# Scale factors of the feed-forward weights made sixteen pairs earlier, and three small operations put in other places

## What is computed

```python
x = x + _layernorm(attn(_layernorm(x)))   # 32 heads of 128, RMS norm over all of q and of k, softmax, Wo
x = x + _layernorm(ffn(_layernorm(x)))
def ffn(x):                               # 8 experts of rank 16
    base = x @ W_base.T + b_base
    gate = softmax(x @ W_gate.T); thr = sigmoid(x @ W_thr.T + b_thr) / 8
    w = where(gate >= thr, gate - thr, 0); w = w / sum(w)
    h = einsum("nd,erd->ner", x, A)
    return base + 2 * einsum("ner,ne,eor->no", h, w, B)
```

## Time and profile before

| | |
|---|---|
| median of three executions | 1068.48 us (1067.88 to 1068.65) |
| the profiled execution | 1073.24 us, of it the profile's span 1071.4 us |
| TensorE busy | 1044.0 us, 97% of the span |
| VectorE, ScalarE, GpSimd busy | 821.3, 762.6, 761.5 us |
| mean granted TensorE clock | 0.993 of full speed |

### The profile page before, as it was taken

One profiled execution on the slowest core, in us unless ns is written; L12 is line 12 of the kernel. 1 busy time (PEld: TensorE's weight loads), 2 busy tenths in 40 slices (PEclk: granted clock), 3 DMA queues, 4 the chain that ended last, 5 costly groups with the idle time before them and its releaser, 6 DMA issues.

```text
span 1071.4 us, 19670 instructions
## 1 busy us (share of the span) xinstructions
PE 1044.0 (97%) x5649; PEld 551.4 (51%) x5649; DVE 821.3 (77%) x1824; ACT 762.6 (71%) x1582; POOL 761.5 (71%) x717
## 2 busy tenths in 40 slices
PE   8999999999999989999999999999999999999897
PEld 5444444444445645556555555555555555544454
DVE  7888766667746778766787887787887887888887
ACT  3676666666657776776787788687787788677756
POOL 2688978788868466775777877877778778645513
PEclk8999999999999999999999999999999999999999
DMA  6679765656664679866577887867878878776702
GB/s 239 172 238 273 258 221 197 230 206 228 205 137 139 199 177 241 236 157 177 138 163 206 183 163 199 165 177 187 194 167 186 197 185 173 210 164 148 186 22 80
DMA packets 312409, 198.86 MB, mean 186 GB/s; under 512 B 275456, under 2 KB 279424, under 8 KB 312320
## 3 DMA queue, kind: packets, MB, share of 16 engines
q1 hardware_dynamic: 304688, 194.24, 68.0%
q10 hardware_dynamic: 7632, 3.57, 1.3%
HBM read 94.98 MB, written 35.68 MB: 122 GB/s over the span
## 4 chain that ended last, share of the span: by engine, by line
PE 80%; DVE 8%; ACT 5%; issue 3%; DMA 2%; POOL 1%; SPq 0%; ACTq 0%; POOLq 0%; DVEq 0%
PE ps L1594 24%; PE ps L1595 23%; PE ps L1596 23%; PE ps L1786 3%; PE ps L1788 3%; PE ps L1787 3%; DVE pair_q L2515 3%; ACT ps L1288 2%; ACT pair_q L1297 1%; DMA pair_k<-pair_q 1%; DVE ps L2501 1%; ACT k_hi L1245 1%; DVE stats L2090 1%; DMA y<-x 0%; DVE ffn_top L2619 0%
## 5 line engine op out<-in xcount | busy, mean ns | idle before, releaser
L2515 DVE SCALAR_TENSOR_TENSOR pair_q<-ps,row_inv,pair_q 128x512 f16<-128x512 f32 x256 | 174.5, 745 | 68.6 <-ACT pair_q L1297 65.0
L1288 ACT ACTIVATE ps<-ps,neg_max 128x512 f32<-128x512 f32 x256 | 168.2, 657 | 76.1 <-DVE ps L2501 76.0
L1594 PE MATMUL ps<-xh,wa_hi 128*128 128x512 f16 x512 | 194.2, 379 | 0.0
L1596 PE MATMUL ps<-xh,wa_lo 128*128 128x512 f16 x512 | 194.2, 379 | 0.0
L1595 PE MATMUL ps<-xl,wa_hi 128*128 128x512 f16 x512 | 194.2, 379 | 0.0
L2501 DVE TENSOR_SCALAR_CACHE_REDUCE ps<-ps,score_down 128x512 f32<-128x512 f32 x256 | 177.0, 753 | 12.2 <-PE ps L1596 11.9
L1297 ACT ACTIVATE pair_q<-ps,row_inv 128x512 f16<-128x512 f32 x256 | 154.5, 688 | 7.8 <-DVE row_inv L2508 7.5
L742 POOL TENSOR_TENSOR acc<-acc,squares 128x512 f32<-128x512 f32 x120 | 151.5, 1284 | 1.6 <-ACT squares L1139 1.6
L1139 ACT ACTIVATE squares<-ps,q_k_bias,qk_down 128x512 f32<-128x512 f32 x128 | 99.3, 784 | 45.9 <-PE ps L1596 31.6
L733 POOL TENSOR_TENSOR qk_out<-q_s,qk_out 128x512 f16<-128x512 f32 x64 | 76.0, 1188 | 53.3 <-ACT qk_out L1148 53.3
L2300 DVE TENSOR_SCALAR qk_out<-ps,k_b,k_g 128x512 f32<-128x512 f32 x64 | 51.8, 809 | 77.1 <-ACT squares L1139 77.1
(11 more groups left out here) (310 smaller groups left out, 2578.3 us busy)
## 6 DMA issues: line engine op xcount, KB each, us to landing
q_k_scratch<-qk_out SPq DMA_DIRECT2D x64, 512.0 KB, 3.6
qk_in<-q_k_scratch SPq DMA_DIRECT2D x64, 512.0 KB, 3.7
wa_stage<-w_qk SPq DMA_DIRECT2D x32, 512.0 KB, 4.3
u_stage<-w_vo SPq DMA_DIRECT2D x32, 512.0 KB, 5.3
wo_stage<-w_vo SPq DMA_DIRECT2D x16, 512.0 KB, 5.2
x_first<-w_vo SPq DMA_DIRECT2D x12, 512.0 KB, 4.5
qk_tops<-qk_top_scratch ACTq DMA_DIRECT2D x27, 128.0 KB, 3.7
y<-x SPq DMA_DIRECT2D x8, 256.0 KB, 6.0
```

What stands on the lines that cost most here:

```text
L1288: act.activation(ps[:, SCORE + i, :], ps[:, SCORE + i, :], ACT.Exp, bias=neg_max[:, sl, i:i + 1], scale=-1.0, accum_out=row_sum[:, sl, i:i ...
L1594: pe.matmul(outp, lhs[0], rhs[0], start=first, stop=False)
L1596: return pe.matmul(outp, lhs[1], rhs[0], start=False, stop=last)
L2515: dve.scalar_tensor_tensor(out=pair_q[:, 1, i, :], in0=ps[:, SCORE + i, :], scalar=row_inv[:, sl, i:i + 1], in1=pair_q[:, 0, i, :], op0=AL ...
```

## The change

On VectorE, the four reductions are done after steps 11, 13, 14 and 15, on base weights that ScalarE loads for this alone into `wv_stage` (two transfers of 512 KB, issued by ScalarE in steps 12 and 14, `load_base`). The load into `wb_stage` in step 52 stays, so `W_base` is loaded twice. SP stores the results in step 49 and loads them in step 50. `last_factors` follows step 52 (`two_pairs` now calls it at `j == 4`). ScalarE's high parts of `W_base` move to the ends of steps 57 and 58, those of the other two to the end of step 60. GpSimd's six splits move into steps 57 to 62, one each. `scores_down` moves from behind the low halves to between `inverses` and the low halves, in every step. In step 2, `maxima` come before `low_wo(0)`, the low halves before `split_v`, and `low_wo(1)` after both.

```diff
@@ SP
+                if j == 1:
+                    sp.wait_ge(ffn_top_ready, 4)
+                    sp.dma_start(ffn_top_scratch[0], ffn_top[:, :]).then_inc(ffn_top_stored, 16)
+                if j == 2:
+                    sp.wait_ge(ffn_top_stored, 16)
+                    sp.dma_start(ffn_tops[:, :, :], ffn_top_scratch.broadcast_to([P, P, 4])).then_inc(ffn_tops_loaded, 16)
             for s in range(4):
                 step(PAIRS - 2, s)
-                if s == 1:
...
-                if s == 2:
...
@@ GpSimd
-            for s in range(4):
-                step(PAIRS - 2, s, 0, more=2)
-            step(PAIRS - 1, 0, 1, more=2)
-            step(PAIRS - 1, 1, 1, weights=False)
-            low_base(0)
-            low_base(1)
-            step(PAIRS - 1, 2, 1, prepare=False, weights=False)
-            low_base(2)
-            low_base(3)
-            step(PAIRS - 1, 3, 1, prepare=False, weights=False)
-            pool.wait_ge(inv_ready, 4 * PAIRS)
...
+            step(PAIRS - 2, 0, 0, more=2)
+            step(PAIRS - 2, 1, 0, late=low_base(0, 2 * PAIRS + 3))
+            step(PAIRS - 2, 2, 0, late=low_base(1, 2 * PAIRS + 4))
+            step(PAIRS - 2, 3, 0, more=4, late=low_base(2, 2 * PAIRS + 6))
+            step(PAIRS - 1, 0, 1, more=5, late=low_base(3, 2 * PAIRS + 8))
+            step(PAIRS - 1, 1, 1, weights=False, late=low_others(0, 2 * PAIRS + 9))
+            step(PAIRS - 1, 2, 1, prepare=False, weights=False, late=low_others(1, 2 * PAIRS + 10))
             step(PAIRS - 1, 3, 1, prepare=False, weights=False)
@@ ScalarE
+            def load_base(k):
+                act.wait_ge(wv_lo_ready, 8)
+                if k:
+                    act.wait_ge(ffn_top_ready, 2)
+                act.dma_start(wv_stage[:, :, :].rearrange("p c n -> p (c n)"),
+                              w_base[:, k:k + 2, :].rearrange("p c n -> p (c n)")).then_inc(wb_loaded, 16)
...
+            step(3, 0, 1, wo_parts(3, 1, 0), beside, part=formed(1, 1, 4))
+            load_base(0)
+            step(3, 1, 1, wo_parts(3, 1, 1), beside, part=formed(1, 1, 5))
+            step(3, 2, 1, wo_parts(3, 1, 2), beside, part=formed(1, 1, 6))
+            load_base(2)
+            step(3, 3, 1, wo_parts(3, 1, 3), part=formed(1, 1, 7))
...
+            after = (None, high_base(0, 1), high_base(2, 3), None)
             for s in range(4):
-                step(PAIRS - 2, s, 0, wo_parts(PAIRS - 2, 0, s), alone=s + 1)
+                step(PAIRS - 2, s, 0, wo_parts(PAIRS - 2, 0, s), alone=s + 1, build=after[s])
-            step(PAIRS - 1, 0, 1, high_base(0, 1), alone=5)
-            step(PAIRS - 1, 1, 1, high_base(2, 3), alone=6)
+            step(PAIRS - 1, 0, 1, nothing, alone=5, build=high_others)
+            step(PAIRS - 1, 1, 1, nothing, alone=6)
@@ VectorE, step
                 inverses(n, sl)
+                if down:
+                    scores_down(n + 1, 2 * p + (s + 1) % 2 + (2 if s == 3 else 0), 1 - sl, (s + 1) % 4 // 2)
                 for i in range(TB):
                     low_halves(n, sl, i)
...
-                if down:
-                    scores_down(n + 1, 2 * p + (s + 1) % 2 + (2 if s == 3 else 0), 1 - sl, (s + 1) % 4 // 2)
@@ VectorE, step 2
+            maxima(2, 0)
             low_wo(0)
-            maxima(2, 0)
-            low_wo(1)
             inverses(2, 0)
-            split_v(4, 6, YB)
             for i in range(TB):
                 low_halves(2, 0, i)
+            split_v(4, 6, YB)
+            low_wo(1)
             scores_down(3, 1, 1, 1)
@@ VectorE, later
             step(2, 3, 0, beside, part=formed(1, 1, 3))
             largest_of_last(2, in_loaded, 16, in_stage[:, :, :].rearrange("p c n -> p (c n)"))
+            step(3, 0, 1, beside, part=formed(1, 1, 4))
+            step(3, 1, 1, beside, part=formed(1, 1, 5))
+            largest_of_base(0)
+            step(3, 2, 1, beside, part=formed(1, 1, 6))
             largest_of_last(3, bt_loaded, 16, bt_stage[:, :])
+            step(3, 3, 1, part=formed(1, 1, 7))
+            largest_of_base(1)
...
-            two_pairs(FORMED, 0, largest_of_base)
+            two_pairs(FORMED, 0, last_factors)
```

More of the change, by code:

```diff
@@ L1058, in _, with low_base, low_others @@
             two_pairs(FORMED, 0, last=True)
[L1059 to L1079 removed]
+            def low_base(c, done):
+                return lambda: split_weights(ffn_hi_ready, ffn_lo_ready, c + 1, wb_lo[:, c, :], wb_stage[:, c, :],
+                                             wb_hi[:, c, :], wb_up[:, :], done)
+            def low_others(k, done):
+                lo, stage, hi, up = ((bt_lo[:, :], bt_stage[:, :], bt_hi[:, :], bt_up[:, :]),
+                                     (in_lo[:, :, 0:IN], in_stage[:, :, 0:IN], in_hi[:, :, 0:IN], ffn_by[:, 1:2]))[k]
+                return lambda: split_weights(ffn_hi_ready, ffn_lo_ready, C + 1 + k, lo, stage, hi, up, done)
+            step(PAIRS - 2, 0, 0, more=2)
[5 more added lines that the diff above has]
+            step(PAIRS - 1, 2, 1, prepare=False, weights=False, late=low_others(1, 2 * PAIRS + 10))
+            step(PAIRS - 1, 3, 1, prepare=False, weights=False)
             def add_ffn(t):
@@ L1465, in last_wv, with high_base, some, high_others @@
                 return some
+            def load_base(k):
[4 more added lines that the diff above has]
+                              w_base[:, k:k + 2, :].rearrange("p c n -> p (c n)")).then_inc(wb_loaded, 16)
+            def high_base(*chunks):
+                def some():
+                    act.wait_ge(ffn_by_ready, 1)
+                    act.wait_ge(wb_loaded, 64)
+                    for c in chunks:
+                        act.activation(wb_hi[:, c, :], wb_stage[:, c, :], ACT.Copy,
+                                       scale=wb_up[:, :]).then_inc(ffn_hi_ready, 1)
+                return some
+            def high_others():
+                act.activation(bt_hi[:, :], bt_stage[:, :], ACT.Copy, scale=bt_up[:, :]).then_inc(ffn_hi_ready, 1)
+                act.activation(in_hi[:, :, 0:IN], in_stage[:, :, 0:IN], ACT.Copy,
+                               scale=ffn_by[:, 1:2]).then_inc(ffn_hi_ready, 1)
             def two_pairs(c, odd, last=False):
@@ L1487, in _ @@
             step(2, 3, 0, wo_parts(2, 0, 3), beside, part=formed(1, 1, 3), build=building(1, 3))
-            for s in range(4):
-                step(3, s, 1, wo_parts(3, 1, s), beside if s < 3 else None, part=formed(1, 1, 4 + s))
+            step(3, 0, 1, wo_parts(3, 1, 0), beside, part=formed(1, 1, 4))
[4 more added lines that the diff above has]
+            step(3, 3, 1, wo_parts(3, 1, 3), part=formed(1, 1, 7))
             with act.Fori(1, FORMED // 2) as i:
@@ L1553, in norm_ffn @@
                                scale=rstd[:, 3, t:t + 1]).then_inc(ffn_normed, 1)
-            step(PAIRS - 1, 3, 1, nothing, prepare=False, between=high_others)
+            step(PAIRS - 1, 3, 1, nothing, prepare=False)
             for t in range(TB):
@@ L2622, in largest_of_base @@
             def largest_of_base(k):
[L2623 to L2642, removed]
-            two_pairs(FORMED, 0, largest_of_base)
+                largest_of_last(k, wb_loaded, 16 * k + 16, wv_stage[:, :, :].rearrange("p c n -> p (c n)"))
             def last_factors():
@@ L2660, in last_factors, with two_pairs @@
                                   ALU.mult, ALU.mult).then_inc(ffn_by_ready, 1)
-            step(PAIRS - 2, 0, 0, alone=1)
+            def two_pairs(c, odd, more=None):
+                for j in range(8):
+                    ends = more and j == 7
+                    step(2 * c + j // 4, j % 4, j // 4, part=None if ends else formed(c, odd, j), alone=0 if ends else None)
+                    if more and j == 4:
+                        more()
+            for s in range(4):
+                step(1, s, 1, plain, to=NT - 1 if s < 3 else None)
+            for s in range(3):
+                step(2, s, 0, plain)
+            step(2, 3, 0, beside, part=formed(1, 1, 3))
             largest_of_last(2, in_loaded, 16, in_stage[:, :, :].rearrange("p c n -> p (c n)"))
-            step(PAIRS - 2, 1, 0, alone=2)
+            step(3, 0, 1, beside, part=formed(1, 1, 4))
+            step(3, 1, 1, beside, part=formed(1, 1, 5))
+            largest_of_base(0)
+            step(3, 2, 1, beside, part=formed(1, 1, 6))
             largest_of_last(3, bt_loaded, 16, bt_stage[:, :])
-            step(PAIRS - 2, 2, 0, alone=3)
-            step(PAIRS - 2, 3, 0, alone=4)
-            last_factors()
+            step(3, 3, 1, part=formed(1, 1, 7))
+            largest_of_base(1)
+            with dve.Fori(1, FORMED // 2) as i:
+                two_pairs(2 * i, 0)
+                two_pairs(2 * i + 1, 1)
+            two_pairs(FORMED, 0, last_factors)
+            for s in range(4):
+                step(PAIRS - 2, s, 0, alone=s + 1)
             step(PAIRS - 1, 0, 1, alone=5)
```

15 lines of the change are left out of this document (removed).

## The result

| | kernel before | changed kernel |
|---|---|---|
| median | 1068.77 us (22 runs, 1067.15 to 1070.60) | 1070.27 us (22 runs, 1067.80 to 1073.22) |
| the profiled execution | 1073.24 us, span 1071.4 us | 1070.17 us, span 1068.4 us |

The ratio is 1.0014, with a 95% interval of 1.0008 to 1.0020: 1.5 us slower, where 1.8 us faster was forecast, and just above the range. Yet the two profiled executions differ by -3.0 us. Medians and profiles point in opposite directions, and that is the question of this study. The spread of the changed kernel is also wider (5.4 us against 3.5).

A forecast was written before the change was run, and what follows sets the result against it. TensorE was taken to bound the loop, VectorE's chain the end of attention. Part 1 at -4.0, part 2 at nothing and part 3 at +2.2 gave -1.8 us from 1068.48: 1066.7 us, range 1062.4 to 1069.8.

The forecast's parts named there:

- The bound and the tail: End of attention: VectorE's chain decides; without the added work, scores of step 56 to 62 take 54.5 us, not 60.3.
- the two port holds: Steps 59 and 60: GpSimd's splits hold up VectorE's `row_inv` at the shared port, 0.6 and 1.0 us, together +1.6.
- The last link, from step 62 to the end, stays as it is: After step 62: the stretch to the end of the kernel was forecast not to change.
- Step 53: the stop: Step 53: TensorE waits 2.2 us for a copy, because `last_factors` after step 52 makes VectorE's maxima 2.43 us later.
- a rival of its own with 0.16: Step 53: the clock falls behind the stop too, costing up to 1.5 us, total 1068.2; chance 0.16.
- Part 2: Every step: `scores_down` moves into a pause where VectorE waits for ScalarE; forecast to change nothing.
- part 1: End of attention: reductions moved to steps 12 to 16, `last_factors` after step 52, high parts and splits earlier; -4.0 us.
- Part 3: Step 2: VectorE's new order delays `low_wo(1)`, on which SP waits before issuing the transposes; +2.2 us, bounds +1.9 and +4.5.
- Landing then took 5.5 us and I keep that: Step 2: the low transposes were assumed to land 5.5 us after starting, as in the first profile.
- The wait of SP for `low_wo(1)`: Step 2: SP waits for `low_wo(1)` until 384.4, so the low transposes begin at 387.0, not 385.07, 1.9 us later.
- ScalarE's wait for the same load: Before step 3's exponentials: low halves of step 3 come at 393.5 to 394.5, ahead of what TensorE needs.
- The slower rival: Loop: `scores_down` held by GpSimd at most steps makes VectorE the bound, 44 steps cost 6.6 us, some 1071.3; chance 0.12.

The follow-up runs named there:

- a_step2_old: The changed kernel with step 2 in VectorE's old order; 1064.89 us, ratio 0.9961.
- a_sp_later: The changed kernel with `load_wo(0)` moved behind step 2 in SP's list; 1070.81 us, ratio 1.0021.
- the second profile of before: The kernel before, run again unchanged for another profile; 1068.97 us, ratio 0.9996, span 1068.3 us.
- b_down: The kernel before with only `scores_down` moved between `inverses` and the low halves in every step; 1067.38 us, ratio 0.9979.
- a_both_54: The changed kernel with `last_factors` after step 54 and, in step 2, `low_wo(0)` and `low_wo(1)` right behind `maxima`; 1063.52 us, ratio 0.9950.

## Why the prediction was wrong

**The bound and the tail: right.** VectorE's round against TensorE's 9.08 was read rightly. Six steps of 9.08 were forecast as 54.5 and are 54.48, in five kernels. Parts 1 and 2 together were forecast at -4.0 and measured -4.2 (-6.3 to -2.0). Counted from the scores of step 53, the forecast had the scores of step 62 at 85.9 us (989.6 - 903.73), and they came at 85.89 (990.98 - 905.09); the low halves of step 62 at best at 91.6 and with the two port holds at 93.2, and they came at 92.77. "The last link, from step 62 to the end, stays as it is" was right as well: from those low halves to the end of the span it is 1071.4 - 1000.87 = 70.53 us before and 1068.4 - 997.86 = 70.54 after.

The holds happened otherwise than forecast. Both fell in step 59, the second one on `scores_down`, each beside a subtraction on GpSimd:

```profile
968.71 1.16 POOL L837 TENSOR_TENSOR wo_lo<-wo_stage,wo_hi 128x512 f16<-128x512 f32 x1
968.89 1.00 DVE L2518 TENSOR_SCALAR row_inv<-row_rec 128x5 f32<-128x5 f32 x1
969.81 1.20 DVE L2411 TENSOR_SCALAR score_down<-rms,exp_scale 128x5 f32<-128x5 f32 x1
969.83 1.16 POOL L888 TENSOR_TENSOR k_lo<-qk_in,k_hi 128x512 f16<-128x512 f32 x1
```

TensorE did not stop for them: VectorE's low halves of step 58 had begun 2.9 us ahead of the scores that need them (960.83, 963.74), and those of step 59 still began 1.9 ahead (970.92, 972.82), where in the kernel before a lead of 0.9 was the one at which TensorE stood waiting (low halves of step 57 at 951.55):

```profile
952.44 0.38 PE L1594 MATMUL ps<-k_hi,qk_in 128*128 128x512 f16 x1 [0.63 <-DVE pair_q L2515]
```

But the lead did not come back. From there VectorE went round in 8.97 to 8.99 us up to step 62, on its own chain:

```profile
960.83 2.73 DVE L2525 SCALAR_TENSOR_TENSOR pair_q<-ps,row_inv,pair_q 128x512 f16<-128x512 f32 x4 [1.12 <-DMA pair_k<-pair_q]
970.92 2.71 DVE L2525 SCALAR_TENSOR_TENSOR pair_q<-ps,row_inv,pair_q 128x512 f16<-128x512 f32 x4
...
997.86 2.73 DVE L2525 SCALAR_TENSOR_TENSOR pair_q<-ps,row_inv,pair_q 128x512 f16<-128x512 f32 x4 [0.62 <-ACT pair_q L1293]
```

So the low halves of step 62 came 6.88 us after their scores and not 5.67: the term for the holds was 1.6, and 1.2 is what was lost (a wait of the low halves of step 58 for a transpose has a part in that, 0.5 us, which the forecast didn't have). Over all fourteen profiles the stretch from these low halves to the end is 70.1 to 70.7 us, while they came 6.9 to 8.1 us after their scores: the end goes with VectorE's chain, as the forecast assumed. No run takes the holds away, so their price at the end isn't shown by itself. The Trainium skill, SBUF — State Buffer, section SBUF: two separate sides, has VectorE and GpSimd lock one port pair for a whole instruction. The rows of step 59 agree with it.

**Step 53: the stop right, its price between two cases.** 2.2 was forecast, 2.01 to 2.23 measured in five profiles. In three the clock stayed up (12.57, 12.59, 12.80 us for the step), in two it fell and the step took 14.25 and 14.26. I had that as a rival of its own with 0.16; it is no either-or of kernels but of executions, 1.7 us in some of them: no profile of the changed kernel itself shows the fall, but `a_step2_old` and `a_sp_later`, which have the same step 53, do. That the changed kernel's times spread wider fits this; the timed runs have no trace, so it isn't shown for them. The Trainium skill, TensorE: Matmul & The Clock Gate, section Part 1: The HAM clock gate, says that the monitor runs free and doesn't start with the kernel. The five profiles are in keeping with that, though they don't prove it: stops of the same length, 2.01 and 2.02, came out both ways.

**Part 2: something alone, with part 1 not to be told.** I costed it at nothing and had its 0.14 us in part 1's round of 8.98. Alone it gives 2.2 us, all in the tail. Together with part 1 steps 56 to 62 went from 55.93 to 54.48, but the profile with both lost as much again to the clock in step 53 (14.25 against 12.80), and in the medians (ratios 0.9967 and 0.9961) no gain can be told.

**Part 3: the step that failed.** "Landing then took 5.5 us and I keep that", "The slow matmuls behind the stall stay", and, for the sum, "That execution lies 4.8 us above the median; the difference of two of them carries over". All three take the one profile of before for what the kernel usually does. It isn't: in it the low transposes of step 2 landed after 5.68 us; in four of the other five profiles with that order it was 4.07 to 4.14 us, TensorE stopped 0.78 to 0.86 us and the clock stayed up. So the usual kernel had neither the long stop nor the slow matmuls, and the change brings both. Against the second profile of before, 17.09 to 23.79 us:

```
stop before attend of step 2    4.85 - 0.86                                +4.0
12 matmuls of attend            (397.73 - 393.02) - (392.36 - 389.78)       +2.1
stop before rows (385.42)       0.92 - 0.33                                +0.6
```

which is 6.7, and 7.2 (5.9 to 8.5) measured alone. So the term of +2.2 in the sum is the one that was mis-sized, and it measured +5.7 to +7.2. What I forecast as +2.2 is right as a difference to the first profile's stop alone (4.85 - 2.41 = 2.44; the whole stretch grew by 3.6 even against that profile), and that was luck, by two errors. On the forecast's clock, 0.76 us behind the changed kernel's, `low_wo(1)` was done at 384.4, just as forecast; but the low transposes went out at 389.7 and not 387.0, mostly since the high ones, issued 1 us behind the two loads, held SP for 3.85 us instead of 1.66; and they landed after 4.04 us instead of 5.5. Some 3.1 of the 4.8 us in which the first profile lay above the median stood exactly in the stretch that the change strikes, and didn't carry over. From the scores of step 0 to the end, the changed kernel's first profile and the second one of before give (1068.4 - 350.41) - (1068.3 - 351.74) = +1.4 us, and the medians +1.5.

**Both ways of part 3.** The wait of SP for `low_wo(1)` was named rightly, and ScalarE's wait for the same load too, but I took the second as harmless since the low halves came "ahead of what TensorE needs". `a_sp_later` shows that it is as dear as the first once that is gone. The cause of both is `low_wo(1)`, which begins 8.93 us after the scores of step 2 (382.87) and not 4.22 (378.92), and `a_both_54` shows that the rest of the new order costs nothing.

**The slower rival** ended on the right side for a wrong reason: the loop isn't bound by `scores_down` (scores 4 to 53 took 0.7 us less than in the second profile of before, where the profiles of all kernels but `a_sp_later`, whose clock was down in step 4, spread by 1.8). Its condition, most steps caught, did not come about: 15 of 49 in the loop. Its time was summed wrongly, too: 1066.7 + 6.6 is 1073.3 and not 1071.3. No rival had step 2 as its place with the kernel before free of a stop.

## What to carry to other kernels

A profile is one execution. Where it lies far above the median, ask first whether the excess stands in the very stretch that the change touches: a stop that is only there in that execution hides what the change would bring on. And where an engine in a cycle has no time in hand, a block of small operations between two links costs: here 2.1 to 2.2 of its 2.6 us, at either of two places, behind step 52 and behind step 54. Cut up and put into the pauses in which the engine waits anyway, it cost nothing that the profile shows.

## What the runs showed of the hardware

- The same SBUF-to-SBUF DMA transpose, issued at the same point of the program, landed after 4.07 to 4.14 us in four executions and after 5.68 and 5.82 in two (from SP's issue to TensorE's first product of it, old order of step 2). With other orders of step 2 it was 3.95 to 4.09 us in seven executions. What makes the difference stays open.
- In step 2, issued 1 us behind two loads of 512 KB, the high transposes held SP's queue for 3.71 to 4.03 us; about 3 us behind them, for 1.64 to 1.73; with no load ahead of them (`a_sp_later`), for 1.37.
- After a stop of TensorE of 2.55 us (`b_down`, step 2) the granted clock stayed at 1.00, the 2.4 GHz level; after one of 2.41 in the same place it was at 0.53; stops of 2.0 went both ways.
